# Third layer of a graph network: links of a chunk's running sum alternate with the joins of the chunk before, on VectorE

## The reference, cut to what matters

```python
m = jax.nn.relu(feat[src]) + EPS
logits = BETA * m
seg_max = jax.ops.segment_max(logits, dst, num_segments=N)
ex = jnp.exp(logits - seg_max[dst])
denom = jax.ops.segment_sum(ex, dst, num_segments=N)
a = ex / denom[dst]
msg = jax.ops.segment_sum(a * m, dst, num_segments=N)
feats = feat + msg
return feats @ W + b
...
x = _layernorm(x + _L1_gnn_ref(...), axis=-1)
x = _layernorm(x + _L2_gnn_ref(x, src, dst, L2_gnn_W, L2_gnn_b), axis=-1)
```

## Time and profile before

| | us |
|---|---|
| median of 3 runs (3713.02 to 3721.47) | 3716.92 |
| the profiled execution | 3727.21 |
| its span, first to last instruction | 3725.5 |
| DVE busy in the span | 2834.9 (76%) |
| POOL busy in the span | 2684.8 (72%) |
| ACT busy in the span | 1861.4 (50%) |
| PE busy in the span | 1745.3 (47%) |

### The profile page before, as it was taken

How to read it: one execution, slowest core, us unless ns; L and a number is a source line. 1 busy time by engine, 2 the same in 40 slices (tenths; PEclk the granted TensorE clock), 3 DMA queues, 4 the chain that set the end, 5 groups by cost and what they waited for, 6 DMA issues and landing times. The chain is left out here.

```text
span 3725.5 us, 39491 instructions
## 1 busy us (share of the span) xinstructions
PE 1745.3 (47%) x8382; PEld 1266.7 (34%) x8382; DVE 2834.9 (76%) x10254; ACT 1861.4 (50%) x3805; POOL 2684.8 (72%) x2760
## 2 busy tenths in 40 slices
PE   5478675877776766754444437777700000000000
PEld 2244313777665655532222226666600000000000
DVE  9899987888876777758999869988865655555565
ACT  8699702776662222224555447777733333333333
POOL 8577776777747777757777747777567777777776
PEclk9799855898887787766666658877855555555555
DMA  1211397665556666646666636555422222222221
GB/s 50 57 40 40 75 291 205 175 168 156 156 139 187 208 212 206 209 129 198 206 206 205 204 123 198 195 193 194 164 82 82 78 78 82 74 82 74 82 78 51
DMA packets 380537, 524.62 MB, mean 141 GB/s; under 512 B 221914, under 2 KB 255983, under 8 KB 380042
## 3 DMA queue, kind: packets, MB, share of 16 engines
q1 hardware_dynamic: 286154, 366.89, 29.8%
q0 software_dynamic: 94144, 155.21, 17.6%
HBM read 230.36 MB, written 291.54 MB: 140 GB/s over the span
## 5 line engine op out<-in xcount | busy, mean ns | idle before, releaser
L1305 POOL DMA_INDIRECT l1b_G<-t,src x391 | 383.3, 980 | 143.9 <-issue 117.1
L1936 POOL DMA_INDIRECT l_G<-t,src x391 | 374.2, 957 | 154.7 <-issue 106.6
L1627 POOL DMA_INDIRECT l_G<-t,src x391 | 377.2, 965 | 149.5 <-issue 118.5
L1305 POOL DMA_INDIRECT l1a_G<-t,src x391 | 376.0, 962 | 149.3 <-issue 116.9
L1951 POOL DMA_INDIRECT out<-O,nidx x392 | 385.3, 983 | 127.7 <-issue 118.0
L2170 PE MATMUL l_psR<-l_diag,l_ones 128*128 128x128 f32 x2 | 0.8, 501 | 993.1 <-DVE l_diag L2034 993.1
L639 POOL DMA_INDIRECT O<-x_pad,nidx x344 | 327.1, 951 | 104.7 <-issue 104.7
L970 POOL DMA_INDIRECT l_G<-xs,src x327 | 312.5, 956 | 99.7 <-issue 97.3
L2170 PEld LDWEIGHTS l_psR<-l_diag,l_ones 128*128 128x128 f32 x2 | 0.5, 310 | 993.2 <-DVE l_diag L2034 993.2
L207 ACT ACTIVATE O<-O,l_shift,l_rstd 128x96 f32<-128x96 f32 x784 | 292.1, 455 | 43.9 <-DVE l_shift L201 43.4
L1480 PE MATMUL l1b_psE<-l1b_G,ident 128*128 128x384 f32 (+1 forms) x198 | 142.2, 820 | 277.8 <-DMA l1b_G<-t,src 277.8
(11 more groups left out here) (351 smaller groups left out, 6278.7 us busy)
## 6 DMA issues: line engine op xcount, KB each, us to landing
h<-l_G SPq DMA_DIRECT2D x96, 392.0 KB, 2.9
t<-l1b_t_out SPq DMA_DIRECT2D x48, 768.0 KB, 3.8
h<-l_G SPq DMA_DIRECT2D x48, 768.0 KB, 3.5
xs<-en_y SPq DMA_DIRECT2D x48, 392.0 KB, 4.0
t<-l_t_out SPq DMA_DIRECT2D x48, 392.0 KB, 4.4
l_H<-t SPq DMA_DIRECT2D x48, 392.0 KB, 3.2
en_y<-x_pad SPq DMA_DIRECT2D x48, 384.0 KB, 5.0
t<-l_tr_out SPq DMA_DIRECT2D x48, 384.0 KB
```

The costliest lines, as they stand in the source:

```text
L1305: pool.indirect_dma_start(tile(c)[:, q, :], None, table, bass.IndirectOffsetOnAxis(k.src[:, at:at + 1], 0))\
L1627: pool.indirect_dma_start(tile(c)[:, q, :], None, table, bass.IndirectOffsetOnAxis(k.src[:, at:at + 1], 0))\
L1936: pool.indirect_dma_start(tile(c)[:, q, :], None, t4, bass.IndirectOffsetOnAxis(k.src[:, at:at + 1], 0))\
```

## The change

In the steps t = 1 to 47 DVE no longer runs the eight joins of chunk t-1 in a row ahead of the chain of chunk t. It runs one link of chunk t, then one join of chunk t-1, and so on eight times. The waits between links stay. In step 0 and from step 48 on nothing is changed.

```diff
+            def chain_and_join(c):
+                S, u = tile(c), (c - 1) % 2
+                dve.wait_ge(gathered.of(c), gathered.by(c))
+                dve.drain()
+                for q in range(Q):
+                    at = STARTS[c] + q
+                    if q:
+                        dve.wait_ge(linked, links(c, q - 1))
+                    before = S[:, q - 1, :] if q else tile(c - 1)[:, Q - 1, :]
+                    dve.scalar_tensor_tensor(S[:, q, :], before, k.cont[:, at:at + 1], S[:, q, :],
+                                             ALU.mult, ALU.add).then_inc(linked if q < Q - 1 else chained, 1)
+                    last = dve.scalar_tensor_tensor(inv[:, u, q, :], shares[:, q, :], k.lastok[:, at - Q:at - Q + 1],
+                                                    k.O[:, at - Q, :], ALU.mult, ALU.add)
+                last.then_inc(joined, 1)
...
-                for c in due(t - 1, LATE):
-                    join(c)
+                paired = 1 <= t < NCH - 1
+                if not paired:
+                    for c in due(t - 1, LATE):
+                        join(c)
...
                 for c in entering(t):
-                    chain(c)
+                    if paired:
+                        chain_and_join(c)
+                    else:
+                        chain(c)
```

## The result

The changed kernel takes 3845.44 us (median of 4 runs, 3844.92 to 3858.23) against 3714.97 us before (4 runs): a ratio of 1.0355, 95% interval 1.0341 to 1.0369. That is 130 us slower, where 120 were forecast (3837 us), inside the range of 3785 to 3900. The profiled execution took 3858.23 us with a span of 3856.5.

A forecast was written before the change was run, and what follows sets the result against it. POOL's gathers were taken to pace the kernel before; afterwards a serial loop would. 46 steps x (12.72 - 10.165) = 117.5, plus 4.8 for the last step, minus 2.6, gave +119.7 us: 3837 us, range 3785 to 3900.

The forecast's parts named there:

- The pair: On DVE, one link and one join overlap by 0.08 us and together take 0.564 us.
- The rival without overlap: On DVE, a join starts only when its link has ended: 0.76 us each pair, 3907 us total; chance 0.08.
- the one with joins hidden: On DVE, joins fit wholly into the links' step: 0.454 us each pair, 3800 us total; chance 0.06.
- The loop: Serial path over DVE, PE and ACT between neighbouring chains' first links: 12.72 us a step against 10.165 before.
- first link to last join: On DVE, eight alternating links and joins, until `joined`: 4.59 us.
- to the end of the `xT` copy: From `joined` through PE's turn and ACT's two copies: 4.23 us, between 3.61 (fast turn) and 4.54 (slow turn).
- to the invert: On ACT, the gap from the end of `copy_x` to the start of the invert: 0.07 us.
- the invert: On ACT, the duration of the invert's two instructions: 1.68 us.
- to the divide: From the inverse's end on ACT to the waiting DVE's divide: 0.03 us.
- to the next link: On DVE, from the divide to the next chain's first link, without joins or gather wait: 2.12 us.
- The term that was mis-sized: From `joined` to the end of `copy_x`, taken at two thirds between fast and slow turns: 4.23 us.
- The shorter first two steps: The first two changed steps have no `copy_x` yet: about 1.3 us less each, -2.6 us in all.

The follow-up runs named there:

- cut at the `xT` copy: The changed kernel with ACT's invert and root moved ahead of the `xT` copy: 3807.99 us, ratio 1.0227 to the kernel before.
- cut at invert and add together and without pairs: Changed kernel with shares in SBUF, invert first on ACT after the joins, joins in a row after the chain, add behind them: 3733.24 us, ratio 1.0040.

## Why the prediction was right

**What bounds the kernel before.** POOL's eight gathers, with DVE half a microsecond behind: shown by the runs with seven gathers (0.9951 before, no change after).

**The pair.** Forecast 0.564 us, measured 0.56 (2571.71 to 2572.27); the last join ends 4.53 us after the first link, forecast 4.59. The rival without overlap (0.76) and the one with joins hidden (0.454) both fall. A link of 0.41 us and a join of 0.31 take 0.56 together.

**The loop.** Its terms as forecast and as in the step shown: first link to last join 4.59 and 4.53; to the end of the `xT` copy 4.23 and 4.76 (2576.24 to 2581.00); to the invert 0.07 and -0.10, since ACT's next instruction starts before the copy's end; the invert 1.68 and 1.67; to the divide 0.03 and 0.02; to the next link 2.12 and 2.07. Together 12.72 and 12.95. That these waits are the cause, and not merely there, the experiments show: cut at the `xT` copy the loop gives back 37 to 48 us, cut at invert and add together and without pairs it gives back all but 17. Two ties hold the invert back, the shared `psT` and its place behind `copy_v` in ACT's queue; no run loosens one of them alone, so what each would cost by itself is not shown.

**The term that was mis-sized** is the clock. In the kernel before, the turn of 1.94 us had a granted clock of 0.50 (2562.78 to 2564.72) and the one of 1.08 had 1.00 (2420.07 to 2421.15). That two thirds of the turns would be slow was my estimate, and no run shows it: the earlier trace rows say only that at least half of the transposes they cover took 421 ns or more, and in the changed kernel all between 2240 and 2790 us took 417 or more. In the step shown that term is 4.76 rather than 4.23, 0.53 more. Of that, 0.31 is the share of slow turns (4.54 instead of 4.23), and 0.22 is the second turn: in the step from which I took 4.54 as all slow, the turn of the normed rows took 1.70 us, and here it takes 1.92, so 4.54 was no upper bound. The other terms give back 0.30 (the pair 0.06, the invert's start 0.17, the invert, the way to the divide and the next link 0.07), so this step is 0.23 longer than forecast, and the mean step 0.17 (12.89): the sum came out closer than its largest miss because the misses have opposite signs. In sums: 46 steps gave 125.1 us where 117.5 - 2.6 = 114.9 were forecast, and the last step 130.3 - 125.1 = 5.2 where 4.8 were; 130.3 instead of 119.7. The shorter first two steps are a second, small miss: I took 1.3 us off each, and they are 12.5 us, 0.4 off the mean. The run with TensorE busy shows that more work in the loop goes with a higher clock (0.92 against 0.73), and what the lower one costs, about 50 us. I took the share of slow turns from the kernel before and did not ask what the change does to it. There TensorE had been idle for 3.24 us ahead of a slow turn and for 1.67 ahead of a fast one; the change lengthens that to 5.45.

**Gathers.** Forecast: POOL waiting 2 to 3 us per chunk with time to spare. Measured 3.0 us in the mean (131.7 in 44 waits) and 3.2 at most, and no effect, by seven gathers and by four buffers. The 4.3 us to landing in that sum rest on little: either trace gives a landing time for only the last three gathers of these chunks (3.3 to 4.4 us before, 2.5 to 3.2 in the changed kernel), so how long a landing takes within the steps is not shown. That the gathers have time to spare rests on the run with seven.

## What to carry to other kernels

Before moving work behind a chain, follow what hangs on its semaphore: the joins were hidden under nothing while they stood early, but they released a turn, two copies and an invert that were hidden under the chain, and 0.9 us of saved VectorE time a step (5.41 less 4.53) came with a step that is 2.7 us longer. A buffer that serves two purposes (here one PSUM tensor for shares and transposes) and an in-order queue tie such steps together, so look for both when an instruction becomes later. And relieving an engine that wasn't the pace-maker gained nothing here, though it showed the highest busy time (DVE 297 us busy instead of 324, ratio 1.0026).

## What the runs showed of the hardware

- A gather of POOL that was under way among VectorE pairs whose operands all lay in SBUF took 3.04 us instead of 0.95, until 0.8 us after the pairs; 1.07 us at the same depth with one operand of the join in PSUM, 0.94 among joins alone. The gathers beside eight links in a row, whose two tensor operands both lie in SBUF, took at most 1.14 us (kernel before, 2240 to 2640 us). What of the alternation makes the difference stays open.
- TensorE's transposes of the joined rows took 421 ns in the median at a granted clock of 0.73, and 273 ns at 0.92 with 24 more transposes a step, which made the kernel about 50 us faster. Idle time just ahead of them does not settle which: 2.25 us in one kernel went with 421 ns, 2.67 us in another with 273.
- One gather costs POOL 1.25 us, 0.95 busy and 0.30 of issue, and eight of them 10.0: with one gather less the step of the kernel before fell to the 9.71 us of VectorE's own list.
